# Attention with a gated mixture of experts on one core: the output projection by half batches and pairs of tiles, and another timetable for the gates

## The reference, cut to what matters

```python
# x: (4, 1024, 256); 8 heads of 128; 8 experts, the best 2 per token
xn = _layernorm(x, axis=-1)
s = _L0_attn_ref(xn, Wq, bq, Wkv, bkv, Wo)          # softmax(q k' / sqrt(128), causal) v, then @ Wo
g = _silu(_L0_ffn_ref(xn, rw, rb, w1, b1, w2, b2))  # two experts per token, weighted and summed
x = x + s * g
```

## Time and profile before

| | |
|---|---|
| median of 3 runs | 1088.56 us (1087.25 to 1088.9) |
| the profiled execution | 1086.89 us, of which 1085.0 us are the span of the profile |
| granted clock of TensorE | 1.00 |
| first `maxima` of head 0 | 482.72 us |
| last `o_tile` begins | 1052.52 us |

### The profile page before, as it was taken

How to read it: one execution, slowest core, us unless ns; L and a number is a source line. 1 busy time by engine, 2 the same in 40 slices (tenths; PEclk the granted TensorE clock), 3 DMA queues, 4 the chain that set the end, 5 groups by cost and what they waited for, 6 DMA issues and landing times.

```text
span 1085.0 us, 25159 instructions
## 1 busy us (share of the span) xinstructions
PE 995.2 (92%) x8734; PEld 783.7 (72%) x8734; DVE 859.1 (79%) x1543; ACT 644.6 (59%) x1360; POOL 324.9 (30%) x339
## 2 busy tenths in 40 slices
PE   1647999999999999998889889999999999999997
PEld 1536888888888898965656667767677677777776
DVE  6885777666766555569999999998999999999971
ACT  3812333233333333348888888878888888888860
POOL 0005999899994200020011102121112111112111
PEclk9999999999999999999999999999999999999999
DMA  8548776766665312137897888998999879898992
GB/s 281 178 192 182 154 186 172 173 175 178 178 171 157 89 50 55 37 102 147 165 162 141 158 159 177 164 149 153 171 185 178 148 147 170 160 173 160 175 183 90
DMA packets 402810, 168.80 MB, mean 156 GB/s; under 512 B 345562, under 2 KB 393252, under 8 KB 402052
## 3 DMA queue, kind: packets, MB, share of 16 engines
q1 hardware_dynamic: 345632, 127.04, 56.1%
q10 hardware_dynamic: 50580, 22.45, 8.6%
q0 software_dynamic: 6480, 17.70, 6.6%
HBM read 51.66 MB, written 30.67 MB: 76 GB/s over the span
## 4 chain that ended last, share of the span: by engine, by line
PE 35%; DVE 13%; DMA 3%; ACT 3%; issue 2%; SPq 0%; ACTq 0%; DVEq 0%
PE b_psS L1144 10%; PE b_psO L1167 10%; PE b_psJ L1183 5%; PE b_psJ L1101 4%; DVE b_ph L1383 4%; DVE b_nmax L1347 4%; DMA b_pT<-b_ph 3%; PE b_psS L1194 2%; PE b_psS L1101 1%; PE b_psO L1169 1%; DVE b_outs L1389 1%; ACT b_pr L1252 1%; ACT b_ph L1282 1%; DVE b_psJ L1356 1%; PE b_psS L1147 1%
## 5 line engine op out<-in xcount | busy, mean ns | idle before, releaser
L847 PE MATMUL psU<-bxT,w_p 128*128 128x256 f16 (+1 forms) x1920 | 287.9, 263 | 13.3 <-DVE w_p L273 10.4
L922 ACT ACTIVATE h<-psU,bias 128x256 f32<-128x256 f32 (+1 forms) x320 | 124.7, 447 | 284.9 <-PE psU L847 192.8
L856 PE MATMUL psY<-w_p,hp 128*128 x1704 | 272.4, 273 | 1.8 <-DVE hp L944 1.3
L1144 PE MATMUL b_psS<-b_kp,b_Q 128*128 128x512 f16 (+3 forms) x1152 | 218.4, 326 | 0.1
L847 PEld LDWEIGHTS psU<-bxT,w_p 128*128 x1920 | 189.1, 98 | 33.8 <-issue 15.1
L1252 ACT ACTIVATE b_pr<-b_psS,b_nmax 128x1024 f32<-128x1024 f32 (+7 forms) x256 | 186.7, 734 | 42.4 <-DVE b_nmax L1347 22.8
L1167 PE MATMUL b_psO<-b_pT,b_vp 128*128 128x256 f16 x1536 | 188.6, 272 | 18.1 <-issue 8.4
L1383 DVE SCALAR_TENSOR_TENSOR b_ph<-b_pr,b_rrec,b_ph 128x1024 f16<-128x1024 f32 (+7 forms) x256 | 199.1, 809 | 0.0
L1282 ACT ACTIVATE b_ph<-b_pr,b_rrec 128x1024 f16<-128x1024 f32 (+7 forms) x256 | 187.0, 768 | 15.9 <-DVE b_rrec L1376 15.6
L942 DVE CAST hp<-h 128x512 f16<-128x512 f32 (+1 forms) x160 | 88.5, 553 | 134.0 <-ACT h L922 127.1
L1347 DVE TENSOR_REDUCE b_nmax<-b_psS 128x1 f32<-128x1024 f32 (+7 forms) x256 | 182.7, 745 | 9.2 <-PE b_psS L1147 7.3
(11 more groups left out here) (181 smaller groups left out, 1029.4 us busy)
## 6 DMA issues: line engine op xcount, KB each, us to landing
wstage<-in_L_ffn_w SPq DMA_DIRECT2D x48, 256.0 KB
expert_rows<-rowx SPq DMA_DIRECT2D x67, 128.0 KB
expert_outputs<-y ACTq DMA_DIRECT2D x31, 256.0 KB
a_x_all<-in_L_attn_x SPq DMA_DIRECT2D x8, 512.0 KB, 9.8
a_w_raw<-in_L_ffn_w SPq DMA_DIRECT2D x4, 1024.0 KB, 6.5
xn_split<-a_xp SPq DMA_DIRECT2D x4, 1024.0 KB, 4.9
xn_turned<-a_xT SPq DMA_DIRECT2D x3, 1024.0 KB, 12.8
b_x_row<-in_L_attn_x SPq DMA_DIRECT2D x24, 128.0 KB, 2.6
```

The lines of the kernel that those rows point to most:

```text
L847: mm = eng.matmul(psU[w % U][:, g % 2, 0:tiles * P].rearrange("p (t r) -> p t r", t=tiles), weight(n, a * W1 + c * H + g * P, P), bxT[n % ...
L856: mm = eng.matmul(psY[n % 2][:, t, :], hp[n % 2][:, a, g, t * P:(t + 1) * P], weight(n, 2 * W1 + (2 * g + b) * D, D), start=(g == 0 and k ...
L922: a = eng.activation(h32[w % 4][:, g, 0:rows], psU[w % U][:, g, 0:rows], ACT.Relu, bias=bias[:, ds(e * HT + 2 * q + g, 1)], scale=1.0 / WS)
L1144: mm = eng.matmul(dst, Q[n % 3][:, a, u * P:(u + 1) * P], kb[:, c, lo:lo + w], start=(kk == 0), stop=(kk == 2 and not last))
```

## The change

Five things change, all in `attention`.
- The output projection goes by half batches: `o_pair(r)` multiplies two tiles by four heads (again 24 matmuls, now into the whole bank), in step 4 of heads 5 to 31 and once at the end, 28 times. For a half batch of first heads, ScalarE copies the bank to a buffer `part` (`o_part`), and this is what frees the bank; for the second half batch, VectorE adds the bank to it (`o_sum`). The copies stand at the start of heads 6 to 9, 14 to 17, 22 to 25, 30 and 31 and at the end; the sums at the start of heads 10 to 13, 18 to 21 and 26 to 29.
- The last batch's first four heads go this way too, so that `rows_out` has only its last four heads left.
- The product with the gate moves to GpSimd: `weighted` and then `added` (`added_last` for the last batch), each on two tiles, 128x512 elements.
- The gates begin at head 4: one tile in each of heads 4 to 29, three in each of heads 30 and 31, none in heads 1 to 3 and none at the end.
- `o_low` of a head's second half comes behind `maxima` in step 0 instead of ahead of it. The input rows of the last batch are loaded in head 8 instead of at the end.

```diff
+    PART, MORE = HEADS // 2, TILES // 2
+    gates = [(5 * n + 1, n - PART) for n in range(PART, NH - 2)]
+    gates += [(5 * n + x, NT - 6 + 3 * (n - NH + 2) + x) for n in (NH - 2, NH - 1) for x in range(3)]
+    gate_at = dict(gates)
...
+        def two_of(r):
+            m, p = r // 4, r % 4
+            return m % 2, 4 * (m // 2) + p
+
+        def bank_free(eng, r):
+            second, g = two_of(r)
+            eng.wait_ge(ot_ if second else oe_, g + 1)
...
-            def o_tile(c):
+            def o_pair(r):
+                m, p = r // 4, r % 4
...
+                eng.wait_ge(al_, 2 * PART * (m + 1))
+                if r:
+                    bank_free(eng, r - 1)
+                h0 = PART * (m % 2)
+                for x in range(2):
+                    t = 2 * p + x
+                    for h in range(h0, h0 + PART):
+                        for kk, (a, e) in enumerate(PASSES):
+                            mm = eng.matmul(psJ[:, x * D:(x + 1) * D], outs[:, a, h, t * P:(t + 1) * P], wo_p[:, e, h, :],
+                                            start=(x == 0 and h == h0 and kk == 0), stop=(x == 1 and h == h0 + PART - 1 and kk == 2))
...
-                        if i == 0 and n >= HEADS + 2:
-                            eng.wait_ge(ot_, n - HEADS - 1)
+                        if i == 0 and n >= PART + 2:
+                            bank_free(eng, n - PART - 2)
...
-            rows_out(0, 0, HEADS - 2)
-            o_tile(TILES - 1)
+            rows_out(0, PART, HEADS - 2)
+            o_pair(NH - PART - 1)
...
-            rows_out(3, 0, HEADS - 1)
+            rows_out(3, PART, HEADS - 1)
...
-            rows_out(2, 0, HEADS - 1)
+            rows_out(2, PART, HEADS - 1)
...
-            rows_out(1, 0, HEADS - 1)
+            rows_out(1, PART, HEADS - 1)
...
+            def o_part(g):
+                eng.wait_ge(om_, 4 * (2 * (g // 4)) + g % 4 + 1)
+                if g >= 4:
+                    eng.wait_ge(oa_, g - 3)
+                eng.activation(part[g % 4][:, :, :].rearrange("p t d -> p (t d)"), psJ[:, :], ACT.Copy, scale=0.5 / WS).then_inc(oe_, 1)
...
+                if i == 0 and n >= PART + 2 and not two_of(n - PART - 2)[0]:
+                    o_part(two_of(n - PART - 2)[1])
...
-            def o_gated(c):
-                g = Gb[c % 2][:, :]
-                eng.wait_ge(G_, turn_of[c] + 1)
-                eng.wait_ge(om_, c + 1)
-                eng.scalar_tensor_tensor(g, psJ[:, 0:D], 0.5 / WS, g, ALU.mult, ALU.mult).then_inc(ot_, 1)
+            def o_sum(g):
+                whole = part[g % 4][:, :, :].rearrange("p t d -> p (t d)")
+                eng.wait_ge(oe_, g + 1)
+                eng.wait_ge(om_, 4 * (2 * (g // 4) + 1) + g % 4 + 1)
+                eng.scalar_tensor_tensor(whole, psJ[:, :], 0.5 / WS, whole, ALU.mult, ALU.add).then_inc(ot_, 1)
...
-                if 6 <= k <= LAST and (k - 1) % 5 in (2, 4):
-                    o_low((k - 1) // 5 - 1, (k - 1) % 5 // 4)
+                if 6 <= k <= LAST and i == 3:
+                    o_low(n - 1, 0)
                 if k < LAST:
                     maxima(k)
+                if 6 <= k <= LAST and i == 0:
+                    o_low(n - 2, 1)
...
+            def weighted(g):
+                eng.wait_ge(G_, max(turn_of[2 * g], turn_of[2 * g + 1]) + 1)
+                eng.tensor_tensor(flat(part[g % 4][:, :, :]), flat(part[g % 4][:, :, :]), flat(G_of(g)), ALU.mult).then_inc(og_, 1)
+                eng.wait_ge(og_, g + 1)
+
+            def added(g):
+                eng.wait_ge(ot_, g + 1)
+                weighted(g)
+                eng.wait_ge(xq[g % 3], 16 * (g // 3 + 1))
+                eng.tensor_tensor(flat(xr[g % 3][:, :, :]), flat(part[g % 4][:, :, :]), flat(xr[g % 3][:, :, :]), ALU.add).then_inc(oa_, 1)
```

More of the change, by code:

```diff
@@ L1029, in attention @@
     B_V, X_PARTS = B_K + 1, 8
-    seq = list(range(TILES, NT)) + list(range(TILES))
-    turn_of = {c: s for s, c in enumerate(seq)}
+    PART, MORE = HEADS // 2, TILES // 2
+    gates = [(5 * n + 1, n - PART) for n in range(PART, NH - 2)]
+    gates += [(5 * n + x, NT - 6 + 3 * (n - NH + 2) + x) for n in (NH - 2, NH - 1) for x in range(3)]
+    gate_at = dict(gates)
+    turn_of = {c: s for s, (_, c) in enumerate(gates)}
+    assert sorted(turn_of) == list(range(NT))
     with ExitStack() as ctx:
@@ L1053, in attention @@
         yg = [sb(f"yg{i}", [P, 2, D], F32) for i in range(3)]
[L1054 to L1057, removed]
+        fb = [sb(f"f{i}", [P, D], F32) for i in range(3)]
+        thb = [sb(f"th{i}", [P, D], F32) for i in range(3)]
+        Gp = [sb(f"G{i}", [P, 2, D], F32) for i in range(4)]
+        part = [sb(f"part{i}", [P, 2, D], F32) for i in range(4)]
+        outs = sb("outs", [P, 2, HEADS, T], F16)
         pT = sb("pT", [P, QT * (QT + 1), P], F16)
@@ L1419, in _ @@
                 n, i = k // 5, k % 5
-                if i == 0 and n >= HEADS + 2:
-                    o_gated(n - HEADS - 2)
+                if i == 0 and n >= PART + 2 and two_of(n - PART - 2)[0]:
+                    o_sum(two_of(n - PART - 2)[1])
                 if k - 1 in jobs.at:
@@ L1433, in _ @@
                     low(k - 2)
-                if k < LAST and n:
-                    if i == 2:
-                        whole_f(seq[n - 1])
-                    if i == 4:
-                        gated(seq[n - 1])
+                if k - 1 in gate_at:
+                    whole_f(gate_at[k - 1])
+                if k - 3 in gate_at:
+                    gated(gate_at[k - 3])
             def closing(s):
@@ L1443, in closing @@
                 eng.scalar_tensor_tensor(g, row_bank[j], 0.5 / WS, g, ALU.mult, ALU.mult).then_inc(of_, 1)
-            whole_f(TILES - 1)
-            gated(TILES - 1)
-            o_gated(TILES - 1)
             o_low(NH - 1, 0)
+            eng.wait_ge(fe_, 4)
             closing(0)
@@ L1501, in stored @@
                 eng.wait_ge(oa_, c + 1)
[L1502 removed]
+                eng.dma_start(of[:, 2 * c:2 * c + 2, :], xr[c % 3][:, :, :]).then_inc(xo[c % 3], 16)
             def inputs(c):
```

115 lines of the change are left out of this document (55 added, 60 removed).

## The result

The changed kernel takes 1091.33 us, the median of 20 runs (1088.43 to 1094.83), and the kernel before 1087.74 us in 20 runs beside it (1085.79 to 1095.13). The ratio is 1.0035 with a 95% interval of 1.0024 to 1.0046: slower by some 3.8 us. A second set, 11 runs beside 34, gave 1.004 (1.0024 to 1.0055). The sum on record was +5.1 us.

What follows compares the result with a forecast made beforehand. VectorE sets the pace in heads 1 to 8, TensorE from head 10. Terms -2.7 + 3.2 + 3.7 + 7.5 - 6.6 = +5.1 us: 1092.0 profiled, 1093.7 median; whole range 1083.5 to 1098.5.

Steps and rivals of the forecast that it cites:

- heads 10 to 13, 18 to 21, 26 to 29 (`o_sum`, GpSimd): Heads with o_sum: VectorE's added work, and low slowed by GpSimd's two instructions, cost +7.5 us; the least certain term.
- The sign: Whole kernel: slower 0.57, same 0.16, faster 0.27; the o_sum and GpSimd term, 7.5 or 1.6 us, was to decide it.
- the rival without contention: Step 0: GpSimd and low don't disturb each other; o_sum costs 1.6, the sum is -3.2, 1085.4 us; chance 0.20.
- The bank: Jobs at head starts in heads 6 to 25 wait until ScalarE's o_high and copy free the bank: +3.7 us.
- the rate on record: VectorE instructions with two SBUF inputs lose 0.84 us for 0.98 us of GpSimd overlap, taken from the experts' part.
- Heads 1 to 4: Three heads lose a gate on VectorE and o_low's wait is covered by maxima: 0.9 us each, -2.7 in all.
- The four `o_pair`: Heads 5 to 8: 96 matmuls, 10.5 us, come back from the end, hidden by 7.3 us of TensorE waits: +3.2.
- The end: Behind the last o_pair 102 projection matmuls remain instead of 174, 17.1 us for 24.94, but it begins later: -6.6 us.
- more trouble: Heads with o_sum: low of step 3 ends late, turned probabilities reach TensorE late, 3 to 5 us more; chance 0.11.

Runs made afterwards that it cites:

- second profile of after: The changed kernel run again unaltered, for a second profile: 1091.02 us, ratio 1.004 to the kernel before.
- first of before: First profile of the kernel before, unaltered: 1086.89 us for the profiled execution, 602.31 us of it attention.
- second profile of before: The kernel before run again unaltered, for a second profile: one run of 1085.33 us, attention 605.98 us.
- first profile: First profile of the changed kernel, unaltered, with half clock at three places: attention 613.45 us; the kernel's median is 1091.33 us.
- GpSimd made small: Changed kernel with GpSimd's weighted, added and added_last over one column in place of 512: 1085.04 us, ratio 0.9988 to the kernel before.
- GpSimd timed: Changed kernel with one more wait, so GpSimd's weighted and added start only after VectorE's low of step 0: 1085.23 us, ratio 0.9993.
- second run with both repairs: Changed kernel with GpSimd's two operations behind low of step 0 and ScalarE's o_part a step earlier, run again: 1078.62 us, ratio 0.9942.

## Why the prediction was right, and where it was off

The differences are those of the second profile of after (no half clock in heads 5 and 30 to 31) against the first of before.

| term | on record | measured |
|---|---|---|
| heads 0 to 4 | -2.7 | -1.44 |
| heads 5 to 9 (`o_pair` 3.2, bank 1.34) | +4.5 | +5.5 |
| heads 14 to 17 and 22 to 25 (bank) | +2.35 | +2.25 |
| heads 10 to 13, 18 to 21, 26 to 29 (`o_sum`, GpSimd) | +7.5 | +5.6 |
| heads 30, 31, the end | -6.6 | -6.7 |
| sum | +5.1 | +5.3 |

The sign was right for the reason given. That the sum is met so closely is in part luck. Heads 0 to 4 and 5 to 9 came out 1.3 and 1.0 us dearer than on record and the heads with `o_sum` 1.9 cheaper, and these errors cancel. The measured sum also depends on the pair of profiles: against the second profile of before it is +1.7, and by the runs the change costs some 3.8 us. The 1093.7 us on record for the median stood on three runs of before (1088.56 us), whose median in 20 runs is 0.8 lower; 1091.33 were measured.

**The sign** hung on GpSimd and `low`, and the rival without contention named the point from which it decides: a `low` of step 0 under 1.5 us. It takes 1.9 to 2.1 us in eleven of the twelve heads (2.4 in head 31), and with that load gone, or moved, the kernel is at 0.999 instead of 1.004, which the runs don't tell from no change. The bank's wait decided the sign as much: with it alone repaired the kernel is at 0.999, too. The rule of the Trainium skill cited on record (the page "GPSIMD Engine Reference", section "Key points") is borne out: `low` and `whole_f`, with two SBUF inputs, are slowed (1.41 to 2.12 us and 0.48 to 1.50), and `maxima` and `o_low`, which read PSUM, keep their 1.22 and 0.74 us under the same instructions.

**Its size** was too large: 5.6 us (7.2 in the first profile) for 7.5. `low` was to take 2.2 us and takes 2.12, but heads 27 and 28 last 18.03 us instead of 18.3. TensorE's own head with `o_sum` and no contention is 17.4 to 17.6 (GpSimd made small), and contention adds 0.4 to 0.6 in these two, not 0.85; 4.4 us in all twelve heads by the table's "GpSimd timed". `low` itself is lengthened by 0.71 us for 0.91 of overlap, where the rate on record gives 0.78, and head 20 hardly at all.

**The bank** was sized well: TensorE's nine waits of 0.39 make 3.5 us, on record 3.7; heads 15, 22 and 23 are 0.39 to 0.40 longer, on record 0.41, and head 14 by 0.30, on record 0.3. Heads 16 and 24 don't fit singly (0.13 shorter and 0.83 longer, on record 0.41 each), only in their sum: head 16 of before held a wait of 0.86 us ahead of its values. What the prediction missed is that this term could be taken back whole and with interest, since the bank's 0.16 us of before goes too: 0.55 a head.

**Heads 1 to 4** were mis-sized by half. Heads 2 and 3 last 16.55 us, not 16.2. Of the two parts, the order of `o_low` gives the 0.5 that stood on record as 0.4. The missing gate, on record 0.5, gives 0.15 in the new order (16.70 with it, 16.55 without) and 0.05 in the old one (17.11 and 17.06): without its gates VectorE waits elsewhere, for ScalarE at the last reciprocal and at the `o_low` of step 3 (0.16 and 0.26 us).

**The four `o_pair`** cost more than 3.2: with the bank term repaired, heads 5 to 9 are 3.9 us longer than before (19.06 + 72.46 against 17.75 + 69.88, in the second run with both repairs, no half clock in head 5).

**The end** came out as computed, but not by its steps alone. In the second profile of after the last `o_pair` begins 1.2 us later behind the start of head 30 than `o_tile` did, on record 1.3, and 17.24 us follow. On record 2.4 of the delay were two whole `low`s lying under `added_last`. In fact `low` loses 1.1 us in head 31 and 0.2 in head 30, since GpSimd is nearly done there when it begins. The rest was made up by delays that weren't in the sum, and no run separates them; all of GpSimd's part is 1.8 us (GpSimd made small). The chance of "more trouble" is what the first profile shows in part: waits of 2.07 us ahead of the values in head 29 and 1.10 in head 30 (0.95 and 1.18 in the second).

## What to carry to other kernels

Before moving elementwise work to GpSimd, look at what VectorE does at that moment: two 1.27 us additions cost it up to 1.1 us when they lie on an operation with two SBUF inputs and nothing when they lie on one that reads PSUM, and one wait that delays GpSimd by an operation can decide it. When an engine's copy is what frees a bank, put it ahead of that engine's other work whose user can wait longer: here a swap of two neighbours on ScalarE gave 5 us. A change that loses 0.4% can hold one that gains 0.6 to 0.7%: cost its parts one by one before undoing the whole.
